# Flamingo block: each pair's last output tile done in the next pair, own PSUM banks for output tiles, the last additions shared

## What is computed

```python
x = x + tanh(g_xattn) * attention(layernorm(x), ctx, ctx)   # 32 heads, 8 key/value heads, width 128, causal
x = x + tanh(g_ffn) * ffn(layernorm(x))                      # I = 1792
# attention(q, k, v) = softmax(mask(Q K^T * 128**-0.5)) V, then @ Wd.T;  Q = q @ Wq.T, K = k @ Wk.T, V = v @ Wv.T
# ffn(x) = (silu(x @ Wg.T) * (x @ Wu.T)) @ Wdown.T, each weight w first multiplied by (su @ sv), rank 4
```

## Time and profile before

| | |
|---|---|
| median of 3 runs | 1487.97 us (1487.6 to 1488.99) |
| the profiled execution | 1488.45 us |
| its span, first to last instruction | 1486.6 us |
| busy: TensorE, VectorE, GpSimd, ScalarE | 98%, 74%, 56%, 43% |
| granted TensorE clock, mean | 0.999 of full speed |

### The profile page before, as it was taken

The page is one execution under the profiler, slowest core; times in us unless marked ns, Lnnn a source line. Parts: engine busy times, 40 slices in busy tenths (PEclk is TensorE's granted clock), DMA queues, the critical chain, the costliest instruction groups (busy, mean ns, idle before and its releaser), DMA issues.

```text
span 1486.6 us, 20638 instructions
## 1 busy us (share of the span) xinstructions
PE 1458.5 (98%) x7322; PEld 1185.6 (80%) x7322; DVE 1100.4 (74%) x1581; ACT 640.0 (43%) x1115; POOL 828.0 (56%) x724
## 2 busy tenths in 40 slices
PE   8999999999999999999999999999999999999998
PEld 8878788888888777777777777777888888888886
DVE  5366777777677777777777778878488887767676
ACT  5445455454444343443343444434344444333332
POOL 5598999998788112111121332234387877666663
PEclk9999999999999999999999999999999999999999
DMA  8476687778987633334333333342012111311121
GB/s 271 153 231 216 217 261 247 251 248 302 330 294 248 240 114 114 114 121 137 125 114 114 114 115 137 135 158 66 22 46 62 43 57 50 121 43 63 45 59 69
DMA packets 116070, 218.02 MB, mean 147 GB/s; under 512 B 9472, under 2 KB 47616, under 8 KB 113920
## 3 DMA queue, kind: packets, MB, share of 16 engines
q1 hardware_dynamic: 115968, 216.70, 43.6%
HBM read 151.13 MB, written 65.54 MB: 146 GB/s over the span
## 4 chain that ended last, share of the span: by engine, by line
PE 85%; DVE 6%; ACT 4%; issue 3%; DMA 1%; POOL 1%; SPq 0%; DVEq 0%; ACTq 0%; POOLq 0%
PE bank L535 65%; PE bank L652 4%; ACT o_hi L1010 3%; PE bank L813 3%; PE bank L812 3%; PE bank L814 3%; PE bank L699 2%; PE bank L679 2%; DVE el L1214 1%; DVE er L1214 1%; PE bank L579 1%; DVE X L1376 1%; DMA c_raw<-in_ctx_t 1%; PE bank L723 0%; DVE xc L1208 0%
## 5 line engine op out<-in xcount | busy, mean ns | idle before, releaser
L1546 POOL TENSOR_TENSOR wd_lo<-wd_raw,wd_hi 128x512 fp32r<-128x512 f32 x64 | 94.9, 1501 | 400.8 <-ACT wd_hi L979 400.8
L535 PE MATMUL bank<-xc,wa_hi 128*128 128x512 f32 x896 | 277.3, 391 | 0.0
L535 PE MATMUL bank<-wd_hi,o_hi 128*128 128x512 f32 x512 | 202.1, 395 | 7.6 <-ACT o_hi L1010 7.6
L535 PE MATMUL bank<-wd_hi,o_lo 128*128 128x512 f32 x512 | 199.7, 390 | 0.0
L535 PE MATMUL bank<-wd_lo,o_hi 128*128 128x512 f32 x512 | 199.3, 389 | 0.0
L535 PEld LDWEIGHTS bank<-xc,wa_hi 128*128 128x128 f32 x896 | 167.7, 188 | 36.0 <-issue 1.1
L535 PE MATMUL bank<-xc,wa_lo 128*128 128x512 f32 x448 | 174.5, 390 | 0.0
L1376 DVE SCALAR_TENSOR_TENSOR X<-bank,tg,X 128x512 f32<-128x512 f32 x224 | 156.4, 741 | 0.0
L1301 DVE TENSOR_TENSOR o_lo<-bank,o_hi 128x512 fp32r<-128x512 f32 x128 | 82.1, 684 | 99.7 <-ACT o_hi L1010 99.7
L535 PE MATMUL bank<-x_hi,wf_hi 128*128 128x512 f32 x392 | 153.1, 391 | 0.0
L535 PE MATMUL bank<-x_hi,wf_lo 128*128 128x512 f32 x392 | 152.6, 389 | 0.0
(11 more groups left out here) (176 smaller groups left out, 3393.3 us busy)
## 6 DMA issues: line engine op xcount, KB each, us to landing
q_scratch<-q_st SPq DMA_DIRECT2D x32, 1024.0 KB, 4.3
q_sb<-q_scratch SPq DMA_DIRECT2D x64, 512.0 KB, 5.8
w_raw<-in_wq SPq DMA_DIRECT2D x32, 512.0 KB, 4.1
wd_raw<-in_wd SPq DMA_DIRECT2D x16, 1024.0 KB, 5.2
f_raw<-ffn_eff_scratch SPq DMA_DIRECT2D x28, 512.0 KB, 3.6
er_raw<-in_sf_r SPq DMA_DIRECT2D x42, 256.0 KB, 3.9
e_raw<-in_wf SPq DMA_DIRECT2D x42, 256.0 KB, 5.3
ffn_eff_scratch<-e_eff SPq DMA_DIRECT2D x42, 256.0 KB, 5.1
```

The lines of the kernel that those rows point to most:

```text
L535: last = pe.matmul(to, a, b, start=(start and n == 0), stop=(stop and n == 3 * len(pairs) - 1), skip_group_check=onto)
L1546: g.tensor_tensor(wd_lo[h % 2][:, e, :], wd_raw[:, e, :], f32(wd_hi[h % 2][:, e, :]), ALU.subtract).then_inc(g_wd, 1)
```

## The change

- Output tiles: `output(u-1, 1)` of a pair is done in the next pair, ahead of `output(u-2, 0)`; in the last pair (p = 31) it stays as well. Banks: even units use bank 1 (t = 0) and bank 6 (t = 1, the bank of even units' scores), odd units bank 0 for both tiles, but bank 1 for the last tile of unit 61; units 62 and 63 as before. The waits follow, with a new one ahead of `scores` of even units.
- VectorE's order in a pair: `out_lo(u-2)`, both `masked_minus_max`, `add_to_x(u-3, 1)`, `out_lo(u-1)`, both `normalised`, `add_to_x` of (u-2, 0), (u-2, 1), (u-1, 0).
- ScalarE's order: `out_hi(u-2)`, `exponentials(u)`, `out_hi(u-1)`, the two `output_hi`, `exponentials(u+1)`.
- The end: ScalarE multiplies tiles 5 to 7 of unit 26 by tanh(g) into the buffers f1, ft1, ft2 (`scaled`), GpSimd adds them to X (`add_scaled`), and VectorE's additions 5 to 7 of unit 27 wait for that. `down(27)` uses all eight banks.

```diff
--- before.py
+++ after.py
@@ -206,6 +206,7 @@
     v_add, v_max, v_sub, v_sum, v_inv, v_p = (sem("v_add"), sem("v_max"), sem("v_sub"), sem("v_sum"),
                                               sem("v_inv"), sem("v_p"))
     v_o, v_y, v_x2s, v_x2lo = sem("v_o"), sem("v_y"), sem("v_x2s"), sem("v_x2lo")
+    a_yf, g_yf = sem("a_yf"), sem("g_yf")
     v_f1, v_f2, v_f21, v_f12, v_m, v_d, v_yf = (sem("v_f1"), sem("v_f2"), sem("v_f21"), sem("v_f12"), sem("v_m"),
                                                 sem("v_d"), sem("v_yf"))
 
@@ -280,7 +281,11 @@
     NPAIR = NU // 2
 
     def output_bank(u, t):
-        return t if u < NU - 2 else 4 + 2 * (u - NU + 2) + t
+        if u >= NU - 2:
+            return 4 + 2 * (u - NU + 2) + t
+        if u % 2 == 0:
+            return 6 if t else 1
+        return 1 if t and u == NU - 3 else 0
 
     def score_bank(u):
         return 6 if u < 2 else 6 + u % 2
@@ -304,6 +309,9 @@
     def d_buffer(n):
 
         return 0 if n % 2 == 0 else 1 if n < 13 else 2
+
+    def down_bank(n, k):
+        return 4 + k % 4 if n < NF - 1 else (0, 1, 3, 4, 2, 5, 6, 7)[k]
 
     def ffn_tile(n, k):
         return 2 * (4 * (n // NJ) + k % 4) + k // 4
@@ -521,7 +529,7 @@
                 sp.dma_start(out[:TT // 2].rearrange("n p d -> p n d"), X[:, :TT // 2, :]).then_inc(d_out, 16)
         load_down(NF - 1)
         for k in range(8):
-            sp.wait_ge(v_yf, 8 * (NF - 1) + k + 1)
+            sp.wait_ge(v_yf, 8 * (NF - 1) - 3 + k + 1)
             t = ffn_tile(NF - 1, k)
             sp.dma_start(out[t], X[:, t, :]).then_inc(d_out, 16)
         sp.wait_ge(d_out, 16 * 9)
@@ -646,6 +654,8 @@
                 pe.wait_ge(a_pt, 1)
             elif u:
                 pe.wait_ge(v_add, u if u < 3 else u - 1)
+            if u >= 4 and u % 2 == 0:
+                pe.wait_ge(v_y, 2 * u - 6)
             for t in range(CT):
                 for b in range(2):
                     cb = 2 * t + b
@@ -707,11 +717,20 @@
                 pe.wait_ge(v_o, 2 * u + 2)
                 pe.wait_ge(g_wd, 4 * (u // 4) + 4)
                 pe.wait_ge(a_wd, 4 * (u // 4) + 4)
-            if 0 < u < NU - 2:
-                pe.wait_ge(v_y, 2 * u + t - 1)
-            elif u == 0:
+            if u == 0 and t == 0:
+                pe.wait_ge(v_t2, NQ)
+            elif u % 2 == 0 and u < NU - 2:
+
+                if t == 0:
+                    pe.wait_ge(v_y, 2 * u - 3)
+                else:
+                    pe.wait_ge(v_add, u + 3)
+            elif u == 1 and t == 0:
                 pe.wait_ge(a_c11, NQ)
-                pe.wait_ge(v_t2, NQ)
+            elif u < NU - 3 or u == NU - 3 and t == 0:
+                pe.wait_ge(v_y, 2 * u - 2 if t == 0 else 2 * u + 1)
+            elif u == NU - 3:
+                pe.wait_ge(v_y, 2 * u - 1)
             three_pass(bank[output_bank(u, t)][:, :],
                        [((o_hi[ob][:, e, t * P:(t + 1) * P], o_lo[o_buffer(u)][:, e, t * P:(t + 1) * P]),
                          (wd_hi[par][:, e, :], wd_lo[par][:, e, :])) for e in range(G)]).then_inc(p_y, 1)
@@ -740,13 +759,16 @@
             weighted_values(u - 1)
             score_transposes(u)
             score_transposes(u + 1)
+            if p > 1:
+                output(u - 3, 1)
             output(u - 2, 0)
             output(u - 2, 1)
             if p in COLUMNS1:
                 pe.wait_ge(v_o, 2 * u)
                 columns2(COLUMNS1[p], (2, 3))
             output(u - 1, 0)
-            output(u - 1, 1)
+            if p == NPAIR - 1:
+                output(u - 1, 1)
             prob_transposes(u)
             prob_transposes(u + 1)
 
@@ -804,11 +826,21 @@
                 half, cols = k // 4, slice(k % 4 * P, (k % 4 + 1) * P)
                 if k % 4 == 0:
                     pe.wait_ge(v_d, 2 * n + half + 1)
-                if 8 * n + k >= 4:
+                if n == NF - 1:
+
+                    if k == 1:
+                        pe.wait_ge(v_f2, NF)
+                    elif k == 2:
+                        pe.wait_ge(v_f21, NF)
+                    elif k == 3:
+                        pe.wait_ge(v_yf, 8 * n - 3)
+                    elif k >= 5:
+                        pe.wait_ge(a_yf, k - 4)
+                elif 8 * n + k >= 4:
                     pe.wait_ge(v_yf, 8 * n + k - 3)
                 else:
                     pe.wait_ge(v_y, 2 * (NU - 2) + k + 1)
-                to = bank[4 + k % 4][:, :]
+                to = bank[down_bank(n, k)][:, :]
                 pe.matmul(to, d_hi[b][:, half, cols], dn_hi[n == NF - 1][:, :], start=True, stop=False)
                 pe.matmul(to, d_hi[b][:, half, cols], dn_lo[n == NF - 1][:, :], start=False, stop=False)
                 pe.matmul(to, d_lo[b][:, half, cols], dn_hi[n == NF - 1][:, :], start=False, stop=True).then_inc(p_yf, 1)
@@ -1069,6 +1101,20 @@
                 a.wait_ge(v_x2lo, 12)
             a.activation(d_hi[d_buffer(n)][:, half, :], bank[2 * half][:, :], ACT.Copy).then_inc(a_d, 1)
 
+        def scaled(k):
+
+            n = NF - 2
+            a.wait_ge(p_yf, 8 * n + k + 1)
+            if k == 5:
+                a.wait_ge(v_m, 2 * NF - 1)
+            elif k == 6:
+                a.wait_ge(v_f12, NF)
+            else:
+                a.wait_ge(g_c22, NF)
+                a.wait_ge(v_f21, NF)
+            a.activation((f1, ft1, ft2)[k - 5][:, :], bank[down_bank(n, k)][:, :], ACT.Copy,
+                         scale=tg[:, 1:2]).then_inc(a_yf, 1)
+
         def ffn(n):
             a.wait_ge(p_f[1], n + 1)
             if n:
@@ -1095,7 +1141,12 @@
                 gate_up_hi(n + 1, 2)
             a.wait_ge(v_f12, n + 1)
             a.activation(bank[2][:, :], bank[2][:, :], ACT.Silu).then_inc(a_silu, 1)
+            if n == NF - 1:
+                scaled(5)
+                scaled(6)
             d_hi_of(n, 1)
+            if n == NF - 1:
+                scaled(7)
             if n in COLUMNS2:
                 x2_hi_of(COLUMNS2[n])
             if n < NF - 1:
@@ -1135,17 +1186,17 @@
             scores_out(u + 1)
             if p > 1:
                 out_hi(u - 2)
+            exponentials(u)
             out_hi(u - 1)
-            exponentials(u)
+            if p in WD_STEP:
+                k, heads = WD_STEP[p]
+                for e in heads:
+                    output_hi(k, e)
             exponentials(u + 1)
             if p in COLUMNS1:
                 x2_columns(COLUMNS1[p], (2, 3))
             if p in SPLIT1:
                 x2_hi_of(SPLIT1[p])
-            if p in WD_STEP:
-                k, heads = WD_STEP[p]
-                for e in heads:
-                    output_hi(k, e)
             if p == F_FIRST:
                 for part in range(3):
                     gate_up_hi(0, part)
@@ -1372,8 +1423,10 @@
         def add_ffn(n, tiles):
             for k in tiles:
                 v.wait_ge(p_yf, 8 * n + k + 1)
+                if n == NF - 1 and k >= 5:
+                    v.wait_ge(g_yf, k - 4)
                 to = X[:, ffn_tile(n, k), :]
-                v.scalar_tensor_tensor(to, bank[4 + k % 4][:, :], tg[:, 1:2], to, ALU.mult, ALU.add).then_inc(v_yf, 1)
+                v.scalar_tensor_tensor(to, bank[down_bank(n, k)][:, :], tg[:, 1:2], to, ALU.mult, ALU.add).then_inc(v_yf, 1)
 
         v.wait_ge(g_const, 6)
         for n in range(2):
@@ -1396,15 +1449,16 @@
         for p in range(1, NPAIR):
             u = 2 * p
             if p > 1:
-                add_to_x(u - 3, 1)
                 out_lo(u - 2)
             masked_minus_max(u)
+            masked_minus_max(u + 1)
+            if p > 1:
+                add_to_x(u - 3, 1)
             out_lo(u - 1)
-            add_to_x(u - 2, 0)
-            masked_minus_max(u + 1)
-            add_to_x(u - 2, 1)
             normalised(u)
             normalised(u + 1)
+            add_to_x(u - 2, 0)
+            add_to_x(u - 2, 1)
             add_to_x(u - 1, 0)
             if p in SPLIT1:
                 x2_lo_of(SPLIT1[p])
@@ -1430,7 +1484,8 @@
                 gated_second(n)
                 add_ffn(n - 1, (4,))
                 d_lo_of(n, 1)
-                add_ffn(n - 1, (5, 6, 7))
+                if n < NF - 1:
+                    add_ffn(n - 1, (5, 6, 7))
             else:
                 d_lo_of(0, 0)
                 gated_second(0)
@@ -1616,6 +1671,11 @@
                 apply2(ROWS2[n - 1])
             if n < NF - 1:
                 down_lo(n)
+
+        def add_scaled(k):
+            to = X[:, ffn_tile(NF - 2, k), :]
+            g.wait_ge(a_yf, k - 4)
+            g.tensor_tensor(to, to, (f1, ft1, ft2)[k - 5][:, :], ALU.add).then_inc(g_yf, 1)
 
         c_sums(0)
         c_lo_of(1)
@@ -1655,6 +1715,8 @@
                     ffn_left_lo(0, part)
         for n in range(NF):
             ffn(n)
+        for k in range(5, 8):
+            add_scaled(k)
 
 # ---- launch: one core; the arrays only laid out for the chip ----
 def kernel(**inputs):
```

## The result

The changed kernel takes **1472.53 us** (median of 4 runs, 1472.04 to 1473.04) against 1487.78 us (4 runs) for the one before, measured with it: ratio 0.9896, 95% interval 0.9883 to 0.9908, 15 us faster. The forecast was 1471.5 with a range of 1468.5 to 1479.5. The profiled execution spans 1470.7 us, 15.9 less.

What follows compares the result with a forecast made beforehand. TensorE, busy 98% of the span, was taken as the bound, its gaps mainly 30 pair waits; 15.0 + 1.1 + 1.8 - 1.4 = 16.5 off 1488.45 gave 1471.95, stated as 1471.5 us, range 1468.5 to 1479.5.

Steps and rivals of the forecast that it cites:

- The cover: Behind the transposes of 30 pairs: late tile's twelve products cut the step from 1.34 to 0.84 us, 15.0 us in all.
- The lower bound of 0.25: Idle time booked to each of 30 pairs' waits, taken as the least gain: 7.5 us.
- rival 1: Behind the transposes: the step is mostly switching, each pair gains only its booked 0.25, time 1479.0; chance 0.10.
- The scores' slack: Even units' scores wait for addition (u-2,1), forecast at 15.5 us into the pair against scores at 16.6: slack 1.0.
- Rivals 2: Scores wait for addition (u-2,1), VectorE's chain 1.2 us longer, scores 0.2 late in 30 pairs: 1477.5; chance 0.10.
- rival 3: Late wd_lo (wd_raw late or GpSimd slow) holds both VectorE products, period 17.3, slower at 1492.5 us; chance 0.04.
- the slack list: Checks of each other engine's new order within a pair: product inputs, banks and copies all ready in time, costing nothing.
- Pair 1: A tile moves out but VectorE keeps its chain to 525.6; scores could start at 524.3: loss 1.4 us, bounds 0 and 2.7.
- Pair 31: TensorE's 1.14 us wait for pt ahead of its last tile goes, as GpSimd's sums come sooner: gain 1.1 us.
- wd_hi and wd_raw: Copies move from 11.6 to 8.8 us into the pair; a late load holds ScalarE 0.5 us at worst, costing nothing.
- The end: Three last additions shared with ScalarE and GpSimd, VectorE left with 8, d_hi 0.2 later: gain 1.8 us, bounds 1.0 and 2.0.
- Rival 4: The late tile itself waits for addition (u-3,0), so attention gains nothing: 1486.5 us; chance 0.02.

Runs made afterwards that it cites:

- experiment 1: The kernel before with one unused VectorE reduction (near 0.7 us) in front of o_lo in pairs 2 to 31: 1503.74 us against 1489.57.
- experiment 2: The changed kernel with an unused VectorE reduction in front of out_lo(u-2): 1472.95 us with one per pair, 1497.73 us with three.
- experiment 3: The changed kernel with the former pair's last tile done ahead of the scores, not behind the transposes: 1547.02 us.
- experiment 8: The changed kernel with tile (0,1) in bank 5: 1471.79 us beside 1471.15 us for the changed kernel.
- experiment 5: The changed kernel with the two wd_hi copies of a pair put back behind exp(u+1): 1471.82 us, one run.
- experiment 7: The changed kernel's end halved: eight banks with all additions on VectorE, 1473.06 us; shared additions with the four old banks, 1472.06 us.
- experiment 4: The changed kernel with VectorE's order of the kernel before under the new TensorE order: 1623.2 us.

## Why the prediction was right

- **What bounds it.** TensorE's issue order, as said: after the change it is idle for 0.8 us of 519. That the table's o_hi was really o_lo is shown by experiment 1, where o_lo moved by 0.54 and the product by 0.53.
- **The cover.** 0.50 a pair was forecast from the unwaited step of the earlier trace rows and 0.46 to 0.47 measured. The step itself came out right (0.85 for 0.84); the other 0.03 are in the 48 products between, 11.00 us where the earlier trace rows gave 10.97. The lower bound of 0.25 from the booked idle time was wrong by half, and rival 1 with it. That the gain is the cover rests on three runs: the same delay costs 0.55 a pair without the tile (experiment 1) and nothing with it (experiment 2), and with the tile elsewhere the step is 1.34 again (experiment 3).
- **The scores' slack**, 1.0 forecast, 1.06 measured by using it up. Rivals 2 and 3 would have needed it gone. In a plain pair of the changed kernel VectorE's first product starts 0.14 ahead of the end of GpSimd's subtractions and still takes its 0.69, so the chain was 0.1 shorter than reckoned. The rest of the slack list held: no other wait appears in a pair.
- **Pair 1**: +1.15 against +1.4. The prediction's own terms add up to 525.5, a loss of 1.2 against its 524.3 and not 1.4, and the first product was held for 0.5 rather than 0.8. It put the whole loss on the scores' wait for an addition; 0.83 goes with that wait (0.76 booked, experiment 8). The other 0.32 stays in experiment 8 too, and there it lies in the probabilities' transposes: from 525.86 to the scores at 527.15 is 1.29 us, against 0.97 in a plain pair, while the second unit's product ends at 526.51.
- **Pair 31**: 1.84 against 1.6: its step behind the transposes had been 1.46 us, not the usual 1.34, and the way from scores to weighted values went from 3.09 to 1.87, 1.22 rather than the 1.14 booked as idle. The reason for the lost wait for pt was half right: GpSimd's sums do come earlier, but experiment 5 shows that they do so without the move of wd_hi. That VectorE's order sufficed for it is read from the times, not shown by a run of its own.
- **wd_hi and wd_raw**: in the changed kernel's profile they cost nothing, as said, and the move bought at most 0.4 us. But the bound was wrong: ScalarE was to stand 0.5 us at worst, from landings of up to 5.9 us, and it stood 0.60 in one pair here and 2.57 in one of experiment 8, a load that landed after 8.0 us and cost that pair 0.35. A late wd_raw is what rival 3 asked for; it came in single pairs, and there one product was held, not both.
- **The end**: 1.89 against 1.8. VectorE is the bound (experiment 7). d_hi starts at 1461.50, right behind the second scaling and 5.77 behind the last gate-up product where it was 5.67: 0.1 later, not 0.2, and that is the difference.
- **Rival 4**, a late tile that itself waits, did not happen where the tile was put; experiment 3 shows that it does happen in front of the scores, and there a pair takes 2 us more than in the kernel before.

The sum missed by 0.6 us of 16.5, and part of that closeness is luck: the 29 pairs gained 0.77 less than forecast, pair 1, pair 31 and the end together 0.58 more. The start's scatter, no part of the forecast, took 0.37. The remaining 0.5 up to the median of 1472.53 is what the forecast took off because the profiled execution before lay above its median; the one after (1472.51) doesn't.

## What to carry to other kernels

When an engine that is otherwise full waits for a short chain of others at one point of every period, move a piece of its own work whose inputs are already there into that point, and then count the chain of each other engine anew to the place where its last result is wanted: here the tile's move without VectorE's new order made the kernel 134 us slower than the one before, and the whole change with it 15 us faster. Price such a wait by the start-to-start distance of the same two instructions with and without it, not by the booked idle time. At the end of a kernel ask which engine has the longest queue of last steps: freeing the other one gave nothing until that queue was shared.

## What was not expected of the hardware

- The step behind the transposes cost more than the table books as idle, and by a fixed amount, not a factor. Against the 0.85 us of the step without a wait it is 0.49 longer where 0.25 is booked (a plain pair), 0.61 where 0.37 is booked (pair 31 of the kernel before), and 1.02 where 0.77 is booked (experiment 1).
- In experiment 4 TensorE ran pair scores in 3.49 us that take 1.95 otherwise. The windows of that profile, over these scores and over the rest of the pair (length, then PE, PEld, DVE, ACT, POOL busy, granted clock, DMA share, GB/s):

```profile
700.79:704.21 3.42, 3.42 (x18) 1.64 (x17) 0.02 (x1) 1.20 (x2) 0.00 (x0) 0.54 0.00 0
704.21:723.87 19.66, 15.54 (x83) 12.06 (x81) 12.22 (x20) 5.57 (x10) 2.55 (x2) 0.99 0.25 80
```

The granted clock was 0.54, near the lower of its two levels (1.2 GHz of 2.4), and 0.99 in the rest. Before it fell TensorE had stood 2.09 us in front of an output tile and 1.11 and 0.91 in front of the probabilities' transposes. The next pair had the same three waits, and its scores ran in 1.95 us, so the waits alone don't tell when it falls. In five of the 30 pairs the scores ran slow; these are 23.07 to 23.13 us long where a plain one is 21.43, together some 8 us of that run's 134. All other kernels here show a mean of 0.998 to 1.000, also the one of experiment 3, whose TensorE waits 1.3 us once a pair.
- Equal programs reached attention between 510.13 and 513.77 us. That scatter of the first stage is larger than most effects of this study, and only stretches show those.
